# One decoder layer on one core: a new unit order, each engine's sequence written anew, and no filler matmuls

## The chip, the core and the metric

The kernel runs on one core of a Trainium2 chip. A core has a matrix engine (TensorE, PE in the profile), a vector engine (VectorE, DVE), a scalar engine (ScalarE, ACT), a general engine (GpSimd, POOL) and a queue that only starts transfers (SyncE, SP). Each engine executes its own instructions in the order in which they are written, and waits for another engine only through a semaphore. The metric is the device time of one launch in microseconds (us).

## The reference

The input has 8 batches of 128 tokens with 256 features. Three sublayers follow one another, each with a residual sum and a layer norm:

```python
x = layernorm(x + attn(x, Wq, Wk, Wv, Wo))       # 16 heads of 128, 4 key/value heads, rotary positions
x = layernorm(x + xattn(ctx, ctx, x, filt, D))   # long convolution of k*v, multiplied by x as the query
x = layernorm(x + ffn(x, W_gate, W_qkv))         # 16 heads of 16, gated top-1 key and value, causal

# attn: q, k, v = x@W.T; rotary on q, k; softmax(q k / sqrt(128)) v; out @ Wo.T
# xattn: kv[i,j] = k_i * v_j per head; y = causal_conv(kv[i,j], filt) + kv*D; out_j = sum_i y[i,j]*q_i
# ffn: indicator = one_hot(argmax(gate)); k_s = indicator.k; v_s = top1.v; softmax(q k_s) v_s
```

The second sublayer of a batch needs the convolutions of all 16 of its heads (the table `y36`) and the finished first sublayer of that batch. The attention does not depend on the convolutions.

## The kernel before

**Units.** The attention is cut into 8 units. A unit is one group of 4 heads with its key/value head (4 groups) for one half of the batches (2 halves of 4 batches). The order is group 0 half 0, group 0 half 1, group 1 half 0, and so on. The four units that add to the first half's residual are therefore units 0, 2, 4 and 6, and its first layer norm comes after unit 6 of 0 to 7.

**What a unit does.** While unit u attends, TensorE computes the projections of unit u+1: `K`, `Q0` to `Q3`, `V`, each 6 matmuls of 512 columns (L377), since operands are split into a high and a low fp32r part. ScalarE copies a projection rotated (`rot`, L854 and L855), VectorE multiplies by the cosine (L1113) and adds (L1126), GpSimd multiplies by the sine (L1574). Per batch k of the unit, TensorE makes `scores` (L408), VectorE takes the row maximum (L1189), ScalarE exponentiates (L888), GpSimd multiplies by the inverse sum (`normalize`, L1605), TensorE transposes (`turn`, L497), multiplies by the values (`values`, L514 to L519, and L510 in the last unit) and by the output weights (`output`, 12 matmuls, L532). VectorE adds the result to `x` (`accumulate`, L1219).

**Convolutions.** They are Toeplitz matmuls (L394), 4 for each unit (`C0` to `C3`), placed among the unit's projections. Projections and convolutions take turns in two PSUM banks (`proj_bank`), so each waits until the one before the last has been read out. GpSimd makes the products `kv` (L1564) and ScalarE copies the results into `y36` (L872).

**Second and third sublayer.** Per batch b: `x1_turn` (L624) transposes the normed x, ScalarE copies it (`mix_query`, L988), 15 `pair_products` (L318, L321) multiply `y36` by it, VectorE sums them (`mix_sum`, L1376), `mix_turn` (L634) transposes back, VectorE adds and norms (`add_mix`, the norm steps L1352 to L1366 with a power on GpSimd, L1667), `x2_turn` (L642) transposes, then `gate_project`, `kv_project`, `query_project`, the gating on VectorE (`gating`, `share`), `key_turn` (L676), `fscores` (L688, L693), row maximum (L1430), exponentials (L1025), `fturn` (L704), `fvalues` (L714), `y_turn` (L752) and the last norm. After the eight units a function `seq(i)` lists what every engine does for step i, in which three or four batches are in work at different stages.

**Around the end of the attention.** Unit 7 has no next unit, so it has only the convolutions `C1` to `C3` and no projections. Into it the first steps of batches 0 to 3 are woven. For batch 0 the pair products are shared: the near distances (`CLOSE`, `NEXT`) on VectorE, the others on GpSimd. There `keep_busy(n)` issues n matmuls of 512 columns on a constant tile (L417), whose results nobody reads: 5, 6, 2, 5 and 6 of them in unit 7 and 2 after it, and 13 more at the very start.

**What sets the order.** Everything is an order written out by hand: a body of one unit per engine, run eight times by `phase_a`, and the steps of `seq(i)`.

```python
                    output(1)
                    values(2)
                    turn(3)
                    x1_turn(2, 0)
                    keep_busy(6)
                    mix_turn(0, 0)
                    values(3)
                    output(2)
                    x2_turn(0, 0)
```

## Time and profile before

| | before |
|---|---|
| time, median of 3 runs | 339.44 us (336.38 to 342.62) |
| span of the profiled execution | 334.2 us |
| median minus that span | 5.2 us |
| TensorE busy | 316.0 us (95%) |
| VectorE, ScalarE, GpSimd busy | 253.1 us, 232.3 us, 198.7 us |
| mean granted TensorE clock | 0.991 |

The span runs from the first to the last instruction of the one profiled execution. A time of its own is not given for that execution; what the launch takes around the span is read as the difference to the median of the runs. An engine's busy time counts execution alone, so the rest of the span is waiting. The profile models the ends of matmuls: a stretch in which PE is busy throughout has no gap between matmuls.

### The profile page before, as it was taken

The numbers are of one execution on the slowest core, as the hardware profiler recorded it, in microseconds if no ns is written. First come the engines' busy times: TensorE is split into PE (matmuls) and PEld (weight loads), VectorE is DVE, ScalarE is ACT, GpSimd is POOL, SyncE is SP. The second block draws the span as 40 slices with busy tenths as digits, with TensorE's granted clock in tenths as the row PEclk, the third lists the DMA queues.
The fourth block names the chain that finished last, engine by engine and source line by source line (L and its number), as shares of the span: only waits on it lengthen the run. The fifth ranks groups of instructions, "written<-read, shape, count | busy, mean of one in ns | idle before, by whom it ended". The sixth has DMA issues, their size and how long they took to land.

```text
span 334.2 us, 6299 instructions
## 1 busy us (share of the span) xinstructions
PE 316.0 (95%) x2099; PEld 245.1 (73%) x2099; DVE 253.1 (76%) x505; ACT 232.3 (69%) x691; POOL 198.7 (59%) x284
## 2 busy tenths in 40 slices
PE   6998999999999999999999999999699999999982
PEld 2786798898898888888889888755366566666641
DVE  2698867857867856876865776989877899998646
ACT  3679578768868957968867865531458777878781
POOL 0679835837844857754665763799790866812102
PEclk9999999999999999999999999999979999999998
DMA  6941010042010031010040000000000000000010
GB/s 178 352 194 63 2 33 0 1 127 66 0 31 0 3 127 64 0 33 0 0 138 4 1 0 2 1 2 1 0 1 2 2 16 3 17 19 18 1 33 31
DMA packets 5616, 13.08 MB, mean 39 GB/s; under 512 B 848, under 2 KB 3024, under 8 KB 5328
## 3 DMA queue, kind: packets, MB, share of 16 engines
q1 hardware_dynamic: 5312, 12.29, 11.0%
q10 hardware_dynamic: 272, 0.39, 0.4%
q8 instruction: 17, 0.28, 0.3%
q14 instruction: 15, 0.12, 0.1%
HBM read 11.63 MB, written 1.05 MB: 38 GB/s over the span
## 4 chain that ended last, share of the span: by engine, by line
PE 77%; DVE 8%; POOL 6%; issue 3%; ACT 2%; DMA 2%; POOLq 0%; DVEq 0%
PE bank L377 19%; PE bank L532 11%; PE bank L408 8%; PE bank L394 6%; PE bank L704 4%; PE bank L693 4%; PE bank L497 4%; PE bank L659 3%; POOL q_rope L318 3%; PE bank L519 3%; PE bank L714 2%; POOL q_rope L321 2%; PE bank L514 2%; PE bank L516 2%; PE bank L688 2%
## 5 line engine op out<-in xcount | busy, mean ns | idle before, releaser
L1605 POOL TENSOR_TENSOR prob<-prob,rden 128x512 f32<-128x512 f32 x32 | 34.1, 1066 | 46.3 <-DVE rden L1196 46.3
L1574 POOL TENSOR_TENSOR t_sin<-rot,sin 128x512 f32<-128x512 f32 x36 | 46.5, 1298 | 22.4 <-ACT rot L855 21.8
L888 ACT ACTIVATE prob<-bank,neg_max 128x128 f32<-128x128 f32 x128 | 45.4, 373 | 0.8 <-DVE neg_max L1189 0.7
L532 PE MATMUL bank<-wo_hi,head_hi 128*128 128x256 f32 x128 | 38.4, 300 | 1.2 <-POOL wo_lo L1599 0.8
L1025 ACT ACTIVATE prob<-bank,fneg_max 128x128 f32<-128x128 f32 x128 | 36.8, 381 | 2.2 <-DVE fneg_max L1430 2.2
L532 PE MATMUL bank<-wo_hi,head_lo 128*128 128x256 f32 x128 | 36.0, 281 | 0.0
L532 PE MATMUL bank<-wo_lo,head_hi 128*128 128x256 f32 x128 | 36.0, 281 | 0.0
L932 ACT CAST head_hi<-bank 128x512 fp32r<-128x512 f32 x32 | 18.8, 588 | 23.9 <-PE bank L519 15.8
L1564 POOL TENSOR_TENSOR kv<-ctxT 128x256 f32<-128x256 f32 (+3 forms) x64 | 35.2, 579 | 0.0
L377 PE MATMUL bank<-x_hi,w_hi 128*128 128x512 f32 x96 | 31.5, 409 | 2.8 <-DVE w_hi L1155 2.0
L408 PEld LDWEIGHTS bank<-k_rope,q_rope 128*128 128x128 f32 x240 | 31.3, 191 | 2.6
L1113 DVE TENSOR_TENSOR t_cos<-bank,cos 128x512 f32<-128x512 f32 x36 | 24.7, 687 | 11.1 <-ACT rot L855 10.5
L318 POOL TENSOR_TENSOR q_rope<-y,rot 128x64 f32<-128x64 f32 (+7 forms) x61 | 31.8, 527 | 2.0 <-ACT rot L988 2.0
L1667 POOL TENSOR_TENSOR rstd<-var_eps,half_pow 128x1 f32<-128x1 f32 (+1 forms) x18 | 10.9, 607 | 36.1 <-DVE var_eps L1361 33.1
L408 PE MATMUL bank<-k_rope,q_rope 128*128 128x128 f32 x240 | 31.6, 274 | 0.0
L1249 DVE TENSOR_TENSOR head_lo<-bank,head_hi 128x512 fp32r<-128x512 f32 x32 | 22.1, 690 | 11.7 <-ACT head_hi L932 11.2
L854 ACT COPY rot<-bank 64x512 f32<-64x512 f32 x40 | 23.4, 585 | 10.6 <-PE bank L377 8.7
L377 PE MATMUL bank<-x_lo,w_hi 128*128 128x512 f32 x96 | 30.0, 394 | 0.3 <-DVE x_lo L1138 0.3
L377 PE MATMUL bank<-x_hi,w_lo 128*128 128x512 f32 x96 | 30.0, 394 | 0.1
L1189 DVE TENSOR_REDUCE neg_max<-bank 128x4 f32<-128x512 f32 x32 | 22.0, 687 | 9.8 <-PE bank L408 9.5
L394 PE MATMUL bank<-kv,toep 128*128 128x288 f32 x96 | 27.2, 405 | 0.0
L1126 DVE TENSOR_TENSOR q_rope<-t_cos,t_sin 128x512 f32<-128x512 f32 x28 | 23.2, 850 | 5.1 <-POOL t_sin L1574 5.1
(132 smaller groups left out, 814.6 us busy)
## 6 DMA issues: line engine op xcount, KB each, us to landing
w_raw<-in_wqkv SPq DMA_DIRECT2D x3, 768.0 KB, 5.9
toep<-in_toep SPq DMA_DIRECT2D x8, 256.0 KB, 3.1
wo_raw<-in_wo SPq DMA_DIRECT2D x4, 512.0 KB, 3.5
x_raw<-in_xt SPq DMA_DIRECT2D x2, 512.0 KB, 5.5
ctxT<-in_ctx SPq DMA_DIRECT2D x1, 1024.0 KB, 4.8
x<-in_x SPq DMA_DIRECT2D x1, 1024.0 KB, 8.9
out<-x SPq DMA_DIRECT2D x8, 128.0 KB, 1.7
wf<-in_wf SPq DMA_DIRECT2D x1, 784.0 KB, 4.5
```

The costliest lines, as they stand in the source:

```text
L318: last = eng.tensor_tensor(pr[:, :, d * HD:d * HD + (n - 1) * (HD + 1) + 1:HD + 1], y[:, :, at:at + n], q[:, :, 0:n], ALU.mult)
L377: last = pe.matmul(out[:, :], wp[:, c, col:col + P], xp[:, j, c, :], start=(c + n == 0), stop=(c == C - 1 and n == 2))
L394: last = pe.matmul(out, toep[:, j, hh, tap:tap + P], kv[:, j, m, hh * NB:(hh + 1) * NB, :], start=(m == 0), stop=(m == lb))
L408: last = pe.matmul(score_bank[k % 2][:, h * P:(h + 1) * P], q_rope[:, j, h, k * P:(k + 1) * P], k_rope[:, j, k * P:(k + 1) * P], start=Tru ...
L532: last = pe.matmul(acc_bank[k // 2][:, (k % 2) * D:(k % 2 + 1) * D], hp[:, k % 2, h * P:(h + 1) * P], wp[:, v % 2, h, :], start=(h + n == ...
L854: act.copy(rot[0:H2, par, :], bank_in[H2:P, :])
L888: last = act.activation(prob[:, k % 2, h * P:(h + 1) * P], score_bank[k % 2][:, h * P:(h + 1) * P], ACT.Exp, bias=neg_max[:, k % 2, h:h + ...
L1025: last = act.activation(prob[:, c % 2, h * P:(h + 1) * P], scored[:, h * P:(h + 1) * P], ACT.Exp, bias=fneg_max[:, c, h:h + 1])
L1113: dve.tensor_tensor(t_cos[:, par, :].rearrange("p (b t) -> p b t", b=BH), bank_in[:, :].rearrange("p (b t) -> p b t", b=BH), cos[:, :].uns ...
L1564: last = pool.tensor_tensor(kv[:, buf, :, :, at:at + n], src[:, :, :, 0:n], src[:, :, :, d:HD], ALU.mult)
L1574: pool.tensor_tensor(t_sin[:, par, :].rearrange("p (b t) -> p b t", b=BH), rot[:, par, :].rearrange("p (b t) -> p b t", b=BH), sin[:, :].u ...
L1605: pool.tensor_tensor(own, own, rden[:, k % 2, :].unsqueeze(2).to_broadcast([P, HG, P]), ALU.mult).then_inc(norm_done, 1)
```

## The change

**The order of the units.** `GROUP_OF` and `HALF_OF` name group and half of each unit. The first half's units are now 0, 2, 4 and 5, so its sums are complete after unit 5; the second half's are 1, 3, 6 and 7. Group 2 is used in unit 4 and again in unit 7, so its projection weights are loaded and split a second time (`W_LOADS`, 5 loads for 4).

**The convolutions.** `CONVS_OF` gives the units 4, 5, 5, 5, 6 and 6 convolutions, beside the first, and the units 6 and 7 none. They still share the two banks.

**The fillers.** The 26 filler matmuls at the end of the attention are gone; the 13 at the start stay.

**The products.** All pair products of all batches are on GpSimd. Their buffer for even batches is the place of `kv`, the copied query `qmix` has a buffer of its own, and the first two `x1_turn` write to another PSUM bank than the later ones.

**The sequences.** The loops are gone. Each engine's whole program is a list of some 370 (TensorE), 320 (ScalarE), 360 (VectorE) and 150 (GpSimd) steps. Steps of batches 0 to 2 now stand in units 6 and 7.

```diff
+GROUP_OF = [0, 0, 1, 1, 2, 3, 3, 2]
+HALF_OF = [0, 1, 0, 1, 0, 0, 1, 1]
+HALF_ENDS = [5, 7]
+W_LOADS = [0, 1, 2, 3, 2]
+W_SPLIT_IN = {0: 1, 2: 2, 3: 3, 5: 4}
-BODY = ["K", "Q0", "Q1", "Q2", "Q3", "C1", "C2", "C3", "C0", "V"]
-LAST = ["C1", "C2", "C3"]
+CONVS_OF = [range(1, 5), range(5, 10), range(10, 15), range(15, 20), range(20, 26), range(26, 32),
+            range(32, 32)]
+ITEMS = [ROPED_ITEMS + [f"C{n}" for n in convs] + ["V"] for convs in CONVS_OF]
-        prod = q_rope[:, :, :, :].rearrange("p n h t -> p n (h t)").rearrange(
-            "p n (a j i) -> p n a j i", j=HD, i=HD)
+        prod = [own.rearrange("p (a j i) -> p a j i", j=HD, i=HD) for own in (
+            kv[:, :, :, :, :].rearrange("p n c a m -> p (n c a m)")[:, 0:C * XH * HD * HD],
+            q_rope[:, 0, :, :].rearrange("p h t -> p (h t)"))]
-        qmix = rot[:, :, 0:D]
+        qmix = sb("qmix", [P, 2, D])
...
-                    values(2)
-                    turn(3)
-                    x1_turn(2, 0)
-                    keep_busy(6)
-                    mix_turn(0, 0)
+            x1_turn(0)
+            values(6, 1)
+            scores(6, 3)
+            turn(6, 2)
+            output(6, 0)
+            output(6, 1)
+            scores(7, 0)
+            x1_turn(1)
+            scores(7, 1)
+            values(6, 2)
+            turn(6, 3)
+            item(6, "V")
+            scores(7, 2)
+            v_turn(7)
+            values(6, 3)
+            output(6, 2)
+            mix_turn(0)
+            turn(7, 0)
+            output(6, 3)
```

**Two places in the order.** TensorE, unit 7, around the transpose `mix_turn` of batch 0 (L634). Before (L510 `values`, L497 `turn`, L624 `x1_turn`, L417 fillers):

```order
L510 MATMUL bank5<-probT,v_last 128x512
L497 MATMUL bank4<-ident,prob 128x128 x4
L624 MATMUL bank0<-ident,x 128x128 x2
L417 MATMUL bank3<-filler 128x512 x6
L634 MATMUL bank0<-ident,t_cos 128x128 x2
```

After, what stands from `scores(7, 0)` (L438) to the transpose of the new values (L411); `mix_turn` of batch 0 comes after 15 more matmuls:

```order
L438 MATMUL bank2<-k_rope,q_rope 128x128 x4
L576 MATMUL bank7<-ident,x 128x128 x2
L438 MATMUL bank3<-k_rope,q_rope 128x128 x4
L527 MATMUL bank5<-probT_hi,v_hi 128x512
L529 MATMUL bank5<-probT_hi,v_lo 128x512
L532 MATMUL bank5<-probT_lo,v_hi 128x512
L509 MATMUL bank4<-ident,prob 128x128 x4
L401 MATMUL bank1<-x_hi,w_hi 128x512 x2
L401 MATMUL bank1<-x_lo,w_hi 128x512 x2
L401 MATMUL bank1<-x_hi,w_lo 128x512 x2
L438 MATMUL bank2<-k_rope,q_rope 128x128 x4
L411 MATMUL bank1<-ident,vT 128x128 x4
```

Between batch 0's `x1_turn` and its `mix_turn` stood fillers and unit 7's steps; now it is the second half of unit 6 with the last projection.

VectorE, from the pair products of batch 0 to their sum (`mix_sum`, L1376). Before (L1189 and L1196 row maximum and inverse, L1249 `head_low`, L1236 copy of the turned probabilities):

```order
L1196 RECIPROCAL rden<-den 128x4
L1345 TENSOR_SCALAR x<-x,mean_var1,rstd1 128x256
L1249 TENSOR_TENSOR head_lo<-bank5,head_hi 128x512
L1236 COPY probT<-bank4 128x512
L318 TENSOR_TENSOR q_rope<-y36,rot 128x32x6
L321 TENSOR_TENSOR q_rope<-y36,rot 128x32x6
L1376 TENSOR_REDUCE t_cos<-q_rope 128x256
L1249 TENSOR_TENSOR head_lo<-bank5,head_hi 128x512
```

After:

```order
L1743 TENSOR_SCALAR x<-x,mean_var1,rstd1 128x256
L1673 TENSOR_REDUCE neg_max<-bank3 128x4
L1680 RECIPROCAL rden<-den 128x4
L1696 TENSOR_TENSOR x<-bank6,x 128x512
L1722 TENSOR_TENSOR head_lo<-bank5,head_hi 128x512
L1715 TENSOR_TENSOR probT_lo<-bank4,probT_hi 128x512
L1780 TENSOR_REDUCE t_cos<-kv 128x256
L1722 TENSOR_TENSOR head_lo<-bank5,head_hi 128x512
```

The sum of batch 0 now stands among steps of unit 6, and no product is left on VectorE.

## Rows read from the trace of the kernel before

**Rows 1.** The page: span, busy time by engine, granted clock in 40 slices.

```profile
span 334.2 us, 6299 instructions
...
PE 316.0 (95%) x2099; PEld 245.1 (73%) x2099; DVE 253.1 (76%) x505; ACT 232.3 (69%) x691; POOL 198.7 (59%) x284
...
PEclk9999999999999999999999999999979999999998
```

**Rows 2.** Windows: length, then busy us (instructions) by engine, clock, DMA.

```profile
49.99:178.80 128.81, 128.81 (x802) 112.52 (x801) 94.39 (x160) 98.73 (x287) 78.48 (x87) 1.00 0.12 38
178.80:233.04 54.24, 52.93 (x318) 41.02 (x317) 43.92 (x87) 30.37 (x100) 41.04 (x65) 1.00 0.01 1
233.04:251.00 17.96, 14.38 (x91) 9.37 (x92) 14.52 (x34) 8.98 (x31) 15.33 (x32) 0.90 0.01 1
...
242.00:246.00 4.00, 4.00 (x18) 3.23 (x16) 2.99 (x10) 1.98 (x7) 4.00 (x10) 0.60 0.00 0
...
284.00:317.00 33.00, 33.00 (x278) 20.91 (x277) 28.10 (x72) 26.34 (x84) 11.70 (x24) 1.00 0.04 14
```

**Rows 3.** Windows again, the filler matmuls of line L417 alone (PE, then PEld).

```profile
178.80:233.04 54.24, 6.60 (x26) 2.47 (x26) 1.00 0.01 1
```

**Rows 4.** The chain that ended last: start us, us, what, in order of time.

```profile
49.99 1.39 PE bank L377 x6
...
110.97 1.40 PE bank L377 x6
112.37 0.89 PE bank L408 x8
113.96 1.46 PE bank L394 x6
115.85 1.42 PE bank L532 x12
...
178.80 1.39 PE bank L377 x6
```

**Rows 5.** Timeline of PE around the attention's end: start, us, instruction, idle before.

```profile
213.86 1.24 PE L417 MATMUL bank<-filler 128*128 128x512 bf16 x5
215.47 0.38 PE L532 MATMUL bank<-wo_hi,head_hi 128*128 128x256 f32 x1 [0.37 <-DVE head_lo L1249]
...
233.04 0.59 PE L688 MATMUL bank<-causal,identb 128*128 128x512 bf16 x2
...
241.50 0.44 PE L624 MATMUL bank<-ident,x 128*128 128x128 f32 x2 [2.33 <-DVE x L1345]
...
248.98 0.44 PE L642 MATMUL bank<-ident,x 128*128 128x128 f32 x2 [0.77 <-DVE x L1366]
```

**Rows 6.** Timeline of DVE in unit 7: batch 0's products on VectorE.

```profile
211.85 1.82 DVE L318 TENSOR_TENSOR q_rope<-y,rot 128x256 f32<-128x256 f32 x2
213.50 0.90 DVE L321 TENSOR_TENSOR q_rope<-y,rot 128x224 f32<-128x224 f32 x1
...
215.94 0.78 DVE L318 TENSOR_TENSOR q_rope<-y,rot 128x192 f32<-128x192 f32 x1
216.55 1.30 DVE L321 TENSOR_TENSOR q_rope<-y,rot 128x192 f32<-128x192 f32 x1
```

**Rows 7.** Costliest groups: line, operation, tiles, count | busy us, mean ns | idle before.

```profile
L1605 POOL TENSOR_TENSOR prob<-prob,rden 128x512 f32<-128x512 f32 x32 | 34.1, 1066 | 46.3 <-DVE rden L1196 46.3
...
L318 POOL TENSOR_TENSOR q_rope<-y,rot 128x64 f32<-128x64 f32 (+7 forms) x61 | 31.8, 527 | 2.0 <-ACT rot L988 2.0
...
L1113 DVE TENSOR_TENSOR t_cos<-bank,cos 128x512 f32<-128x512 f32 x36 | 24.7, 687 | 11.1 <-ACT rot L855 10.5
...
L1126 DVE TENSOR_TENSOR q_rope<-t_cos,t_sin 128x512 f32<-128x512 f32 x28 | 23.2, 850 | 5.1 <-POOL t_sin L1574 5.1
...
L1376 DVE TENSOR_REDUCE t_cos<-q_rope 128x256 f32<-128x2048 f32 x8 | 18.2, 2275 | 0.0
```

**Rows 8.** Timeline, the last instruction before the final transfer.

```profile
331.70 0.41 DVE L1366 TENSOR_SCALAR x<-x_raw,mean_var,rstd 128x256 f32<-128x256 f32 x1 [0.44 <-POOL rstd L1667]
```

More of the change, by code:

```diff
@@ new lines, in _ @@
+            scores(1, 0)
+            item(0, "C4")
+            item(0, "V")
+            turn(0, 3)
+            output(0, 2)
+            scores(1, 1)
+            values(0, 3)
+            v_turn(1)
+            item(1, "K")
+            scores(1, 2)
+            item(1, "Q0")
+            turn(1, 0)
+            scores(1, 3)
+            item(1, "Q1")
+            output(0, 3)
+            turn(1, 1)
+            values(1, 0)
+            item(1, "Q2")
+            item(1, "Q3")
+            turn(1, 2)
@@ new lines, in _ @@
+            scores(2, 3)
+            item(2, "Q2")
+            item(2, "Q3")
+            output(1, 2)
+            values(2, 0)
+            turn(2, 1)
+            output(1, 3)
+            item(2, "C10")
+            item(2, "C11")
+            values(2, 1)
+            turn(2, 2)
+            item(2, "C12")
+            scores(3, 0)
+            item(2, "C13")
+            values(2, 2)
+            turn(2, 3)
+            output(2, 0)
+            item(2, "C14")
+            item(2, "V")
@@ new lines, in _ @@
+            output(6, 3)
+            values(7, 0)
+            turn(7, 1)
+            scores(7, 3)
+            x2_turn(0)
+            turn(7, 2)
+            values(7, 1)
+            output(7, 0)
+            gate_project(0)
+            values(7, 2)
+            output(7, 1)
+            turn(7, 3)
+            query_project(0)
+            x1_turn(2)
+            kv_project(0, 0)
+            mix_turn(1)
+            kv_project(0, 1)
+            values(7, 3)
+            output(7, 2)
+            key_turn(0)
@@ new lines, in _ @@
+            output(7, 3)
+            x2_turn(1)
+            fscores(0, 0)
+            gate_project(1)
+            x1_turn(3)
+            kv_project(1, 0)
+            kv_project(1, 1)
+            fturn(0, 0)
+            fscores(0, 1)
+            mix_turn(2)
+            fturn(0, 1)
+            fvalues(0, 0)
+            query_project(1)
+            key_turn(1)
+            fturn(0, 2)
+            x1_turn(4)
+            fscores(1, 0)
+            x2_turn(2)
+            fvalues(0, 1)
@@ new lines, in _ @@
+            fturn(0, 3)
+            fvalues(0, 2)
+            gate_project(2)
+            x1_turn(5)
+            fscores(1, 1)
+            fturn(1, 0)
+            kv_project(2, 0)
+            mix_turn(3)
+            kv_project(2, 1)
+            fvalues(0, 3)
+            query_project(2)
+            fturn(1, 1)
+            y_turn(0)
+            key_turn(2)
+            fvalues(1, 0)
+            fscores(2, 0)
+            x2_turn(3)
+            fturn(1, 2)
+            fvalues(1, 1)
@@ new lines, in _ @@
+            gate_project(3)
+            fturn(1, 3)
+            x1_turn(6)
+            fvalues(1, 2)
+            kv_project(3, 0)
+            fturn(2, 0)
+            fscores(2, 1)
+            fvalues(1, 3)
+            kv_project(3, 1)
+            mix_turn(4)
+            query_project(3)
+            fturn(2, 1)
+            y_turn(1)
+            key_turn(3)
+            fvalues(2, 0)
+            fturn(2, 2)
+            fscores(3, 0)
+            x2_turn(4)
+            fvalues(2, 1)
@@ new lines, in _ @@
+            fvalues(2, 2)
+            gate_project(4)
+            fturn(2, 3)
+            x1_turn(7)
+            kv_project(4, 0)
+            fturn(3, 0)
+            fscores(3, 1)
+            fvalues(2, 3)
+            kv_project(4, 1)
+            query_project(4)
+            mix_turn(5)
+            fturn(3, 1)
+            y_turn(2)
+            key_turn(4)
+            fvalues(3, 0)
+            fscores(4, 0)
+            x2_turn(5)
+            fturn(3, 2)
+            fvalues(3, 1)
@@ new lines, in _ @@
+            gate_project(5)
+            fvalues(3, 2)
+            kv_project(5, 0)
+            fturn(3, 3)
+            fscores(4, 1)
+            fturn(4, 0)
+            kv_project(5, 1)
+            fvalues(3, 3)
+            query_project(5)
+            mix_turn(6)
+            fturn(4, 1)
+            key_turn(5)
+            fvalues(4, 0)
+            y_turn(3)
+            fscores(5, 0)
+            x2_turn(6)
+            fturn(4, 2)
+            fvalues(4, 1)
+            gate_project(6)
@@ new lines, in _ @@
+            fturn(4, 3)
+            kv_project(6, 0)
+            fvalues(4, 2)
+            fscores(5, 1)
+            fturn(5, 0)
+            kv_project(6, 1)
+            fvalues(4, 3)
+            query_project(6)
+            mix_turn(7)
+            fturn(5, 1)
+            key_turn(6)
+            fvalues(5, 0)
+            y_turn(4)
+            fscores(6, 0)
+            x2_turn(7)
+            fturn(5, 2)
+            fvalues(5, 1)
+            gate_project(7)
+            fvalues(5, 2)
```

1972 lines of the change are left out of this document (1299 added, 673 removed).

## The prediction

> **What bounds the kernel now.** I read the page first: TensorE is busy for 316.0 of 334.2 us, all other engines for 76% or less [rows 1]. That share alone doesn't say that TensorE is the limit in every stage, so I cut the span into windows at places the chain gives. From 49.99 to 178.80 us, which are units 1 to 5 (the K projection of unit 1 and that of unit 6 [rows 4]), TensorE is busy for 128.81 of 128.81 us [rows 2]: 25.76 us a unit, no gap, and the chain runs through its matmuls. Nothing but less TensorE work can shorten this stage. The steady part of the later sublayers is of the same kind: 33.00 of 33.00 us from 284 to 317, with VectorE at 28.10 (85%) [rows 2]. What is left are the start, the end, and the passage between the two stages. In the passage, from 178.80 to the first `fscores` at 233.04 [rows 5], TensorE is busy for 52.93 of 54.24 us [rows 2], but 6.60 us of that are 26 fillers whose results nobody reads [rows 3]. They stand in front of waits: the five at 213.86 are followed by 0.37 us of idleness for VectorE's `head_lo` [rows 5]. The useful work is 52.93 - 6.60 = 46.3 us, and 7.9 us are lost. In the next stretch, to 251.00, TensorE is busy for 14.38 of 17.96 us: 3.6 us idle, of which 2.33 us wait for the norm of batch 4 and 0.77 us for that of batch 2 [rows 2, 5]. Behind the long wait the clock falls, to 0.60 over 242 to 246 [rows 2], so that 1.6 us of those 4 are lost as well. **The whole passage loses 7.9 + 3.6 + 1.6 = 13.1 us. That is what the change can give back.**
>
> **The passage, first part.** The same work stands there as before, less 7 convolutions (C1 to C3 of unit 6, C0 to C3 of unit 7, 22 matmuls), which move ahead. Six take 1.46 us on the chain [rows 4], so 22 take 5.4 us, which are paid in units 0 to 5 instead and cancel. That leaves 46.3 - 5.4 = 40.9 us for TensorE. VectorE had 43.92 us there [rows 2] and loses the products of batch 0, 1.82 + 0.90 + 0.78 + 1.30 = 4.8 us [rows 6], so it has 39.1 us, 96% of TensorE's. In the steady stage 85% went with no wait at all, and before, the passage ran at 43.92 / 54.24 = 81% with 7.9 us lost; 96% in order, with every fourth or fifth step waited for, will not be free. GpSimd gets those products: a batch's 15 cost it about 15 x 0.527 = 7.9 us by the mean of the dearer kind [rows 7], and one `normalize` of 1.07 stands between them [rows 7]. With the sum on VectorE, 2.28 us [rows 7], the path from `x1_turn` to `mix_turn` of batch 0 is 7.9 + 1.1 + 2.3 = 11.3 us, and copies and handovers. TensorE has as cover three `output` (4.3 us), four `scores` (3.6), one projection (1.4) [rows 4], three `values` and four short transposes, together some 12.8 us if I put those seven at half a us each. Cover and path are equal to within about a us, so a small wait is likely there, and another at `key_turn` of batch 0, where gating and `share` on VectorE have only 2 `kv_project`, a `values` and one `output` over them. Bounds of what comes back as new waits: nothing (the 40.9 us are dense) and all 7.9 us. I take 3.0, nearer to dense, since the products leave VectorE and real work replaces the fillers. **Term: -4.9 us.**
>
> **The passage, second part.** The second half's statistics now stand on VectorE ahead of the first `fscores` maximum, not behind it, and `x1_turn` of batch 4 stands behind three `fturn` and two `fscores`. The wait of 2.33 us [rows 5] and the slow clock behind it lose their cause. But `key_turn` of batch 1 waits for `gating` and `share` that stand behind a sum of 2.28 us. Bounds: -5.2 and 0. I take 1.7 back. **Term: -3.5 us.**
>
> **The dense units.** Before, units 1 to 5 had no wait, so here the new order can only lose. A convolution or projection needs its bank free, which took two `rot` copies and a cosine product of 0.69 us [rows 7] behind the projection before the last, against one projection of 1.40 us in between [rows 4]: two projections back to back with none between wait, and in the new list they stand in pairs with a `scores` or `turn` between the pairs, as before. Total work rises by 5.4 us of convolutions over these units, with the same share of the other engines. The trace has no such unit. The low bound is 0. For the high one I take 1 us a unit over six, the size of the wait for the norm [rows 5]. Nearest is the stage itself, with none in 128.81 us [rows 2]. **Term: +1.0 us.**
>
> **Edits at nothing.** The fifth weight load is hidden: its split costs ScalarE and VectorE under 2 us each in unit 5, where VectorE had 94.39 of 128.81 us to do over five units [rows 2]; if the cover fails, it is 2 us of wait. The load itself has a unit of 25.76 us to land in. SyncE's queue carries it behind two Toeplitz loads, which wait for convolutions that are now early. The start has the same steps in another order, and the tail's last chain ends in the same apply at 331.70 [rows 8]; its norms of batches 6 and 7 only swap with a short scale. I put both at 0, with 1 us either way.
>
> **A rule that speaks against it: the clock.** The trace shows full speed through all of the fillers, and 0.60 only behind the 2.33 us of idleness [rows 2, 5]. The Trainium skill ("TensorE: Matmul & The Clock Gate", Part 1) puts it as "the default state is throttled, and activity releases the throttle", so fillers have a use of their own. By the trace alone, waits of up to 0.37 us leave the clock up [rows 5], and mine are of 1 us or less, so the sum has nothing for it; by the rule, a spell of waits costs as one below does.
>
> **Another: the port.** VectorE's cosine product reads PSUM and SBUF and takes 687 ns; the addition (L1126) reads SBUF twice and takes 850 ns [rows 7]. That difference is there while GpSimd works beside it. The Trainium skill ("SBUF — State Buffer", Who interferes with whom) says that a tensor_tensor with both inputs in SBUF contends with GpSimd's reads. By the rows, five additions of unit 6 beside busier GpSimd work cost 5 x 0.16 = 0.8 us at most more, which is inside the 3.0 us; by the rule, each could wait for a whole product of 0.5 us, 2.6 us in all.
>
> **The sum.** -4.9 - 3.5 + 1.0 = -7.4 us on a span of 334.2: 326.8 us. The median of the runs lies 5.2 us above that span, so the time is 339.44 - 7.4 = 332.0 us, 2.2% less. A measurement of this kernel can tell about 2%, 6.8 us, from no change; the forecast lies on that line.
>
> **Rivals.**
> (a) *Everything comes back.* The sum of losses is 13.1 us, and nothing new arises. For it: GpSimd and ScalarE have room, and the first half's residual is complete a unit earlier. Against it: VectorE at 96%. With at most 1 us of new waits the time is 339.4 - 12.1 = 327.3.
> (b) *The gain turns into new waits.* VectorE is the passage's engine, and units with six convolutions wait for banks. Then 3 of the 13.1 us stay gained by the passage's two parts, after all 7.9 and 2 us return, and the dense units lose another 2: 339.4 - 3.2 + 2 = 338.2. For it: a list in order with each engine over 90% has no slack, and the dense stage has nothing to win. This is also the case in which the change removes the fillers and not what they covered.
> (c) *Slower: the clock.* One mechanism: at the passage, waits without fillers between them bring TensorE to 1.2 GHz, as at 242 us. One such fall costs its wait of 2.3 and 1.6 us of slow work, 3.9 us. It starts to decide when a wait gets as long as the 2.33 us one; four falls between units 6 and batch 2, with (b)'s waits, give 339.4 - 1.2 + 15.6 = about 354, two give 346. Against it: the waits that I find are about 1 us.
>
> **How the numbers follow.** The forecast (332, itself between 329 and 335.5) has 0.47, (a) 0.15, (b) 0.30, (c) 0.08. Faster by over 2% means below 332.6: all of (a) and 0.34 of the forecast, 0.49. Within 2%: the rest of the forecast and (b), 0.43. Slower by over 2%: (c), 0.08. The range leaves out half of (c) and the ends of (a) and (b): 326 to 341.
>
> **What would show it.** Right: no idleness of TensorE over 1.2 us between K of unit 6 and the first `fscores`, that stretch 43 to 45 us long; units 1 to 5 dense in TensorE, 134 us with their convolutions; clock 1.00 after 240 us. Wrong in the first term: VectorE busy throughout with TensorE waiting for `head_lo` or the turned probabilities. Wrong in the third: waits for cosine products or `rope` sums in units 1 to 5. Wrong in the clock: slices under 9 in the passage. What would upset all is work that I take as equal and isn't: the steady stage's 33.00 of 33.00 us would have to become longer.

## The result, and the profile after

| | before | after |
|---|---|---|
| time, median | 338.5 us (20 runs, 335.99 to 342.78) | 339.5 us (20 runs, 338.26 to 342.06) |
| ratio to before, 95% interval | | 1.006 (1.003 to 1.008) |
| span of the profiled execution | 334.2 us | 336.5 us |
| TensorE busy | 316.0 us | 312.7 us |
| VectorE, ScalarE, GpSimd busy | 253.1, 232.3, 198.7 us | 262.9, 231.3, 204.7 us |

The forecast of 332.0 us and its sign were wrong: the time rose by 0.6%, which the 20 runs of each tell apart from no change, and which is far inside 2%. Rival (b), 338.2 us, comes nearest by the time. A run's time is 1.8 to 1.9 us longer than its own span in every run that lists both (338.36 and 336.5 us for the profiled execution of after). So the profiled execution of before, 334.2 us of span, was one of its fastest; the profiled one of after is among its fastest too, and the two spans, 2.2 us apart, can be compared.

The page of after (span, busy time, granted clock, the chain by engine) answers to [rows 1]:

```profile
span 336.5 us, 6269 instructions
...
PE 312.7 (93%) x2073; PEld 241.0 (72%) x2073; DVE 262.9 (78%) x502; ACT 231.3 (69%) x693; POOL 204.7 (61%) x289
...
PEclk9999999999999999999999999999999999999997
...
PE 36%; DVE 23%; issue 15%; POOL 14%; ACT 8%; DMA 3%; POOLq 0%; DVEq 0%; ACTq 0%
```

The slow slice of before (7, near 242 us) is gone, as forecast. But VectorE has become 9.8 us busier although the change takes five instructions of batch 0's products (4.8 us [rows 6]) off it, and GpSimd, VectorE and "issue" hold half of the chain.

Windows of after, at the places of [rows 2], the first of them without a gap in before and with 5.0 us of idle TensorE now (length, then busy us and instructions by engine, clock, DMA):

```profile
51.15:193.53 142.38, 137.37 (x837) 117.68 (x836) 106.57 (x168) 103.63 (x305) 86.23 (x94) 1.00 0.12 40
193.53:239.05 45.52, 43.08 (x270) 35.03 (x269) 41.32 (x80) 26.06 (x86) 36.08 (x55) 1.00 0.01 2
239.05:257.00 17.95, 17.32 (x123) 10.54 (x122) 17.04 (x39) 12.99 (x45) 17.16 (x38) 1.00 0.01 1
```

I cut both traces at the same work: the first matmul of a unit's K projection, and the first `fscores`. Of before these cuts lie at 49.83, 178.64 and 233.04 us. 22 matmuls of convolutions count 5.35 us [rows 4], and in after one `output` (12 matmuls, 1.42 us [rows 4]) still stands behind the cut at 51.15.

| stretch | before | after | moved work | left over | forecast |
|---|---|---|---|---|---|
| start and unit 0 | 49.83 | 51.15 | -1.42 | +2.7 | 0 |
| units 1 to 5 | 128.81 | 142.38 | +6.77 | +6.8 | +1.0 |
| passage to the first `fscores` | 54.40 | 45.52 | -5.35 | -3.5 | -4.9 |
| from there to the end | 101.20 | 97.44 | 0 | -3.8 | -3.5 |
| sum | 334.2 | 336.5 | 0 | +2.2 | -7.4 |

So the passage did what it was to do, 7.3 of the forecast 8.4 us. Ahead of it 9.5 us were lost where 1.0 was expected. Of the 6.8 us in units 1 to 5, 5.0 are idle time of TensorE (142.38 - 137.37); the rest lies inside its busy time. What TensorE waited for in after, whole span (us in total, times, the longest):

```profile
PE bank L423 <- DVE t_cos L1594: 2.3, 3, 1.0
PE bank L438 <- DVE q_rope L1607: 2.2, 3, 1.2
PE bank L470 <- POOL q_rope L2295: 1.6, 2, 1.1
...
PE bank L401 <- DVE t_cos L1594: 1.4, 4, 0.5
PE bank L401 <- DVE x_lo L1620: 1.3, 1, 1.3
```

Convolutions (L423) wait for cosine products, scores (L438) for sums: the words of the prediction for "wrong in the third". And the groups, as in [rows 7]:

```profile
L2287 POOL TENSOR_TENSOR t_sin<-rot,sin 128x512 f32<-128x512 f32 x36 | 47.3, 1324 | 29.8 <-ACT rot L1128 24.0 <-DVE q_rope L1607 3.5 <-DVE k_rope L1607 2.1
L2315 POOL TENSOR_TENSOR prob<-prob,rden 128x512 f32<-128x512 f32 x32 | 35.5, 1114 | 49.4 <-DVE rden L1680 49.4
L1607 DVE TENSOR_TENSOR q_rope<-t_cos,t_sin 128x512 f32<-128x512 f32 x28 | 33.4, 1214 | 1.8 <-POOL t_sin L2287 1.7
...
L1594 DVE TENSOR_TENSOR t_cos<-bank,cos 128x512 f32<-128x512 f32 x36 | 24.3, 683 | 7.5 <-ACT rot L1128 6.7
```

The same 28 sums went from 850 to 1214 ns, 10.2 us more of VectorE; the cosine product, with one input in PSUM, stayed at 683. With K's eight there are 36 sums. I sorted them by what GpSimd did meanwhile: before, 16 ran beside nothing and took 0.69 us, after only 3; beside a sine product alone 12 of after took 1.28 in the mean, beside `kv` alone 9 took 0.97. The longest took 2.03 us before and 2.40 in after, both beside GpSimd's `wo_lo`.

**One place in full.** The longest pair of waits, in unit 3. TensorE, VectorE and GpSimd of after (start, us, instruction, idle before):

```profile
119.73 1.24 PE L423 MATMUL bank<-kv,toep 128*128 128x288 f32 x4 [0.96 <-DVE t_cos L1594]
121.70 0.75 PE L423 MATMUL bank<-kv,toep 128*128 128x288 f32 x2 [0.73 <-DVE t_cos L1594]
```

```profile
114.55 0.68 DVE L1594 TENSOR_TENSOR t_cos<-bank,cos 128x512 f32<-128x512 f32 x1
115.16 0.67 DVE L1722 TENSOR_TENSOR head_lo<-bank,head_hi 128x512 fp32r<-128x512 f32 x1
115.75 1.63 DVE L1634 SCALAR_TENSOR_TENSOR toep<-anti,dcoef,toep 128x128 f32<-128x128 f32 x2
117.34 1.74 DVE L1607 TENSOR_TENSOR q_rope<-t_cos,t_sin 128x512 f32<-128x512 f32 x1
119.00 0.68 DVE L1594 TENSOR_TENSOR t_cos<-bank,cos 128x512 f32<-128x512 f32 x1
119.72 1.33 DVE L1607 TENSOR_TENSOR q_rope<-t_cos,t_sin 128x512 f32<-128x512 f32 x1
120.97 0.68 DVE L1594 TENSOR_TENSOR t_cos<-bank,cos 128x512 f32<-128x512 f32 x1
```

```profile
113.17 2.74 POOL L2277 TENSOR_TENSOR kv<-ctxT 128x160 f32<-128x160 f32 x5
115.86 2.68 POOL L2287 TENSOR_TENSOR t_sin<-rot,sin 128x512 f32<-128x512 f32 x2
119.22 1.27 POOL L2287 TENSOR_TENSOR t_sin<-rot,sin 128x512 f32<-128x512 f32 x1 [0.69 <-DVE q_rope L1607]
```

C15 needs the bank that Q2's cosine product frees. That product (119.00) stands behind the skip matrices and behind Q1's sum. The sum waits for nothing more, but runs beside a sine product and takes 1.74 us. The sines are late because `kv` (2.74 us) stands ahead of them. VectorE works without a gap here, on steps nobody is waiting for yet, while TensorE waits. Three candidates are left, two in these rows and one beside them: the **order** on VectorE and GpSimd (theory A), the **port** that two engines share (theory P), and that five or six convolutions in a unit are too many wherever they stand (theory C).

### The profile page after: what moved, and what is told of

Read it like the earlier page. It is cut to its first block, busy times and chain, and to the rows that moved or that the text cites. A ratio compares the mean times of both kernels' runs of the same rounds, so it can differ in the third digit from the quotient of the medians.

```text
span 336.5 us, 6269 instructions
## 1 busy us (share of the span) xinstructions
PE 312.7 (93%) x2073; PEld 241.0 (72%) x2073; DVE 262.9 (78%) x502; ACT 231.3 (69%) x693; POOL 204.7 (61%) x289
## 4 chain that ended last, share of the span: by engine, by line
PE 36%; DVE 23%; issue 15%; POOL 14%; ACT 8%; DMA 3%; POOLq 0%; DVEq 0%; ACTq 0%
PE bank L401 5%; DVE q_rope L1607 5%; PE bank L548 5%; PE bank L423 4%; ACT prob L1163 4%; PE bank L438 4%; DVE t_cos L1594 2%; POOL kv L328 2%; PE bank L659 2%; PE bank L617 2%; POOL t_sin L2287 2%; DVE head_lo L1722 2%; PE bank L670 2%; POOL kv L331 2%; ACT rot L1128 2%
## 5 line engine op out<-in xcount | busy, mean ns | idle before, releaser
L2315 POOL TENSOR_TENSOR prob<-prob,rden 128x512 f32<-128x512 f32 x32 | 35.5, 1114 | 49.4 <-DVE rden L1680 49.4
L2287 POOL TENSOR_TENSOR t_sin<-rot,sin 128x512 f32<-128x512 f32 x36 | 47.3, 1324 | 29.8 <-ACT rot L1128 24.0
L401 PE MATMUL bank<-x_hi,w_hi 128*128 128x512 f32 x96 | 33.0, 425 | 3.4 <-DVE w_hi L1641 1.5
L1607 DVE TENSOR_TENSOR q_rope<-t_cos,t_sin 128x512 f32<-128x512 f32 x28 | 33.4, 1214 | 1.8 <-POOL t_sin L2287 1.7
L438 PE MATMUL bank<-k_rope,q_rope 128*128 128x128 f32 x240 | 31.5, 276 | 2.2 <-DVE q_rope L1607 2.2
L438 PEld LDWEIGHTS bank<-k_rope,q_rope 128*128 128x128 f32 x240 | 29.9, 191 | 4.6 <-DVE q_rope L1607 3.5
L2277 POOL TENSOR_TENSOR kv<-ctxT 128x256 f32<-128x256 f32 (+7 forms) x64 | 33.1, 553 | 0.0
L401 PE MATMUL bank<-x_lo,w_hi 128*128 128x512 f32 x96 | 29.9, 393 | 1.3 <-DVE x_lo L1620 1.3
L423 PE MATMUL bank<-kv,toep 128*128 128x288 f32 x96 | 27.6, 410 | 2.5 <-DVE t_cos L1594 2.3
L401 PE MATMUL bank<-x_hi,w_lo 128*128 128x512 f32 x96 | 29.8, 392 | 0.0
L1163 ACT ACTIVATION_READ_ACCUMULATOR prob<-bank,neg_max 128x1 f32 x128 | 27.3, 213 | 0.0
L548 PEld LDWEIGHTS bank<-wo_hi,head_hi 128*128 128x128 f32 x128 | 24.1, 189 | 3.5 <-DVE head_lo L1722 2.0
```

The lines of the kernel that those rows point to most:

```text
L401: last = pe.matmul(out[:, :], wp[:, c, col:col + P], xp[:, j, c, :], start=(c + n == 0), stop=(c == C - 1 and n == 2))
L423: last = pe.matmul(out, toep[:, j, hh, tap:tap + P], kv[:, j, m, hh * NB:(hh + 1) * NB, :], start=(m == 0), stop=(m == lb))
L438: last = pe.matmul(score_bank[k % 2][:, h * P:(h + 1) * P], q_rope[:, j, h, k * P:(k + 1) * P], k_rope[:, j, k * P:(k + 1) * P], start=Tru ...
L548: last = pe.matmul(acc_bank[k // 2][:, (k % 2) * D:(k % 2 + 1) * D], hp[:, k % 2, h * P:(h + 1) * P], wp[:, g % 2, h, :], start=(h + n == ...
L1163: last = act.activation(prob[:, k % 2, h * P:(h + 1) * P], score_bank[k % 2][:, h * P:(h + 1) * P], ACT.Exp, bias=neg_max[:, k % 2, h:h + ...
L1607: dve.tensor_tensor(dst, t_cos[:, par, :], t_sin[:, par, :], ALU.add).then_inc(rope_done, 1)
```

## The experiments

Times are medians; the ratio is to runs of the kernel before, made beside them on the same chip. "Units 1 to 5" is K of unit 1 to K of unit 6. At before's density they take 128.81 + 5.35 = 134.2 us with the seven convolutions; after has 142.38 - 1.42 = 141.0.

### 1. The change's steps in before's unit

The same steps as after, each as often: its unit order, convolutions, and its lists from unit 6 on. The start and units 0 to 5 are written in the pattern of before's unit, on all four engines, TensorE included. Unit 3 on VectorE, after (-) and mixture (+):

```diff
-prob_low 0; cos K; cos Q0; prob_low 1; add K; add Q0; cos Q1; head_low 0; add_skip 4; add Q1; cos Q2;
-add Q2; cos Q3; accumulate; add Q3; head_low 1; row_max 3
+cos K; prob_low 0; row_max 2; cos Q0; head_low 0; add K; add Q0; cos Q1; add Q1; invert 2; add_skip 4;
+cos Q2; prob_low 1; row_max 3; cos Q3; head_low 1; add Q2; add Q3
```

> The same steps as in the changed kernel, in another order up to the end of unit 5: the start and units 0 to 5 follow the unit body of the kernel before (with the extra convolutions put between its own), units 6 and 7 and all behind them are those of the changed kernel. Theory A (the new order of the dense units and of the start makes the waits): units 1 to 5 go from 142.4 us back to about 134, the start and unit 0 give back 2 to 3 us, the passage stays at 45.5; span 336.5 - 10 = 326 to 328. Rival (five or six convolutions in a unit, or the new unit order with its fifth weight load, cost the time whatever the order): units 1 to 5 stay above 139, span 332 to 336.

Measured: 340.75 us, ratio 1.005 (0.999 to 1.011), span 336.4; no gain. But the loss sat elsewhere. The start was back at before's (K of unit 1 at 49.64), the mean sum fell from 1.197 to 0.942 us, and units 1 to 5 took 143.8 us with two waits of convolutions that had not been in after:

```profile
95.54 0.72 PE L423 MATMUL bank<-kv,toep 128*128 128x288 f32 x2 [1.82 <-issue]
...
180.62 1.30 PE L423 MATMUL bank<-kv,toep 128*128 128x288 f32 x2 [2.80 <-issue]
```

"issue" names no releaser. On GpSimd five `kv` products run from 178.70 to 180.51, until just before C28 at 180.62: C12 and C28 begin new pairs (3 and 7), whose `kv` products I had placed too late. This run didn't decide between A and C.

### 2. The same with three placements mended

```diff
 # GpSimd
-unit 2: normalize(3, 0), pairs(4)      unit 5: pairs(7, 0:3), normalize(5, 3), pairs(7, 3:)
+unit 2: pairs(4), normalize(3, 0)      unit 4: pairs(7), normalize(5, 0)
 # TensorE and ScalarE, unit 2: C12 a slot later, then C13 and C14 behind values(2, 3)
```

> The kernel before's way of laying out a unit for the start and units 0 to 5, with the change's distribution of the convolutions, and the change's lists for units 6, 7 and behind. It differs from the first such mixture only in where GpSimd's kv products of pairs 4 and 7 stand (a unit's tail earlier) and in one convolution of unit 2 that stands a slot later. Theory A (the order of the steps inside a unit causes the loss, no property of more convolutions in fewer units): the two waits of 1.82 us at 95.5 and 2.80 us at 180.6 go, and what followed them; from K of unit 1 to K of unit 6 it takes 134.5 to 136.5 us, against 140 in the first mixture, span 330 to 332, ratio to before 0.988. Theory C (six convolutions in a unit leave VectorE or the banks behind, wherever they stand): the same waits turn up at other places, 139 to 141 us, span 335 to 336, ratio 1.00.

Measured: 332.42 us, ratio 0.985 (0.979 to 0.991), span 330.6, as A had them. Both waits were gone. Units 1 to 5 took 137.8 us, 3.6 over full density and midway between A's and C's figures; the "140" that the expectation gives for the first mixture was a slip for 143.8, on which C's figure hung. From K of unit 6 to the end it equals after to within 0.2 us (143.1 and 143.0). **So three placements inside the units are worth 6.0 us, and after's own steps in this order take 5.9 us less of span than in after's (330.6 for 336.5), where after had lost 2.2 us against before: order is the larger part of what was lost.** Against after, 2.9 us of it lie at the start and in unit 0 and 3.2 in units 1 to 5 (141.0 to 137.8); 0.2 go back behind them. The order of every engine differs between the two, so this doesn't say which engine's counted. C isn't dead: 3.6 us remained, of which TensorE is idle for 1.7 (137.80 - 136.12).

```profile
49.70:187.50 137.80, 136.12 (x825) 116.37 (x823) 100.01 (x166) 103.73 (x298) 83.58 (x96) 1.00 0.13 42
187.50:233.05 45.55, 43.06 (x270) 35.03 (x269) 41.31 (x80) 27.18 (x92) 36.02 (x55) 1.00 0.00 1
```

### 3. The port alone: one swap

In experiment 2 one VectorE split ran beside a GpSimd one, both on SBUF alone:

```profile
131.26 2.40 POOL L2309 TENSOR_TENSOR wo_lo<-wo_raw,wo_hi 128x1024 fp32r<-128x1024 f32 x1 [4.53 <-ACT wo_hi L1114]
...
131.95 2.52 DVE L1620 TENSOR_TENSOR w_lo<-w_raw,w_hi 128x768 fp32r<-128x768 f32 x1 [0.99 <-ACT w_hi L1108]
```

```diff
 # ScalarE, end of unit 3
-split_wo(2)
 split_w(3, 1)
+split_wo(2)
```

> The second mixture with one swap in ScalarE's list: at the end of unit 3 it splits the projection weights (w_hi) ahead of the output weights (wo_hi), so that VectorE's w_lo no longer runs beside GpSimd's wo_lo. In the second mixture this one w_lo took 2.52 us beside GpSimd's 2.40 us one, where the eleven others took 0.95 to 1.09, and the values of unit 4 then waited 0.16 and 0.40 us for the turned probabilities, on either side of a late t_cos. Theory P (two engines on SBUF operands at once cost VectorE the difference, and that cost reaches TensorE where a step is waited for soon): this w_lo takes 0.95 to 1.1 us, unit 4 takes 27.5 to 28.3 us for 28.96, K of unit 1 to K of unit 6 136.4 to 137.2 us for 137.8, span 329.2 to 330.0. Rival (the 2.52 us are only a coincidence of a busy DMA or of the weights' own arrival): w_lo stays above 2 us. Second rival (the time is absorbed by slack): w_lo is short and unit 4 stays at 28.8 to 29.0.

```profile
131.00 0.96 DVE L1620 TENSOR_TENSOR w_lo<-w_raw,w_hi 128x768 fp32r<-128x768 f32 x1
...
131.99 2.40 POOL L2309 TENSOR_TENSOR wo_lo<-wo_raw,wo_hi 128x1024 fp32r<-128x1024 f32 x1 [5.26 <-ACT wo_hi L1114]
```

Measured: 331.67 us, ratio 0.983 (0.978 to 0.989), span 329.8; unit 4 took 28.25 us for 28.96. The split fell from 2.52 to 0.96 us, the level of the other w_lo splits (nine, not the eleven of the expectation; 0.95 to 1.08 us). So P is shown as the cause of those 1.6 us of VectorE's time. Of what TensorE got, 0.7 us, it isn't the only cause: the swap also starts the split 0.95 us sooner, so it ends 2.5 us sooner (131.96 for 134.47), and the two weren't separated. By its span this is the fastest of all kernels here, ahead of before (334.2) and after.

### 4. The port taken out of the sums

The cosine product goes back to its PSUM bank and the sum reads it there, so the sum has one SBUF input. The bank is then held until the sum.

```diff
-dve.tensor_tensor(t_cos[:, par, :]..., bank_in, cos, ALU.mult)
-dve.tensor_tensor(dst, t_cos[:, par, :], t_sin[:, par, :], ALU.add)
+dve.tensor_tensor(bank_in[:, :]..., bank_in, cos, ALU.mult)
+dve.tensor_tensor(dst, bank_in[:, :], t_sin[:, par, :], ALU.add)
```

> The changed kernel, but the cosine product is written back into its PSUM bank and the addition reads it there, so it has one input in SBUF and not two; the bank comes free behind the addition and not behind the cosine product. Port theory: additions of 690 ns with GpSimd busy beside them or not, VectorE 10 to 12 us less busy, units 1 to 5 down from 142.4 to 137 or less, unless the banks held longer (0.7 us and more each) take it back. Order theory: nothing gained, and the longer hold costs; units 1 to 5 at 142 to 150.

```profile
L1609 DVE TENSOR_TENSOR q_rope<-bank,t_sin 128x512 f32<-128x512 f32 x28 | 18.5, 681 | 1.6 <-POOL t_sin L2289 1.6
```

Measured: 381.84 us, ratio 1.134 (1.125 to 1.143). All sums are short (681 ns for 1214) beside the same GpSimd work, so the second SBUF input is what lengthens them. The time says how much more a held bank costs than a long sum: units 1 to 5 took 171.2 us, where neither theory had more than 150. TensorE waited for banks behind K's and the queries' sums 14 times on L401 alone (16.0 + 13.8 us), and the clock's mean fell to 0.947. The Trainium skill ("SBUF — State Buffer", Who interferes with whom) says that a VectorE instruction with two SBUF inputs contends with a GpSimd instruction that reads SBUF, and that one with at most one, outside VectorE's two-port modes, doesn't; the runs agree, 0.66 to 0.69 us for all 36 sums here against up to 2.40 us in after.

### 5. Less, and more, on GpSimd

After, with only the shortest `kv` product of each pair from pair 2 on (the other products, and so part of the second sublayer's result, are left out):

```diff
                 for d in ...:
+                    if n >= 2 and d < HD - 1:
+                        continue
```

> The changed kernel with less work on GpSimd in units 1 to 5: of the eight kv products of each convolution pair from the third on, only the shortest is computed (the second sublayer's result is not the reference's). Nothing else moves. Port theory (VectorE's additions with both inputs in SBUF are held up by GpSimd's work): the mean addition falls from 1214 ns to 1000 or less, and units 1 to 5 lose part of their waits, 142.4 to 139 or 140. Order theory (VectorE's steps simply stand late in the list, or banks come free late): additions change, but units 1 to 5 stay within 1 us of 142.4.

Measured: 337.77 us, ratio 1.002 (0.998 to 1.006), span 334.8; mean sum 1.109 us for 1.197, units 1 to 5 1.5 us shorter. Most of `kv` out of the way gives back 1.5 of the 6.8 us, a little beyond the order theory's 1 us and short of P's figures (a mean of 1.0 or less, 139 to 140 us). Most of what stayed of the collisions is with the sines.

Before, with the products of distance 2 and more made a second time:

```diff
+                    if d >= 2:
+                        pool.tensor_tensor(kv_again[..., at - 15:at - 15 + n], src[..., 0:n], src[..., d:HD], ALU.mult)
```

> The kernel before, in which GpSimd makes its kv products of distance 2 and more a second time into a tile that nobody reads: GpSimd is busier beside the same VectorE work, TensorE's order is untouched. Theory P (VectorE's additions of two SBUF tiles are lengthened by GpSimd's tensor_tensor beside them): the mean addition rises from 0.87 to 1.0 us or more. Whether that alone costs the dense units time: by P as the whole cause, units 1 to 5 grow from 25.76 to 26.5 us each or more and the span to 338 or more; by A, with the addition's slack in before's order, they stay within 0.2 us of 25.76 wherever GpSimd's own work isn't late, and the span stays within 1.5 us.

Measured: 347.78 us, ratio 1.030 (1.023 to 1.037), span 347.4, units 0.9 and 1.6 us longer by turns, unit 0 5.5. The mean sum stayed at 0.88 us, so this doesn't bear on P, and my expectation of 1.0 failed: the extra products stood where VectorE made no sums. What grew was another thing, 8.2 us of idleness before the convolutions (L395), where before had none: 0.9 of it the profile puts down to `kv`, and 7.3 to "issue", which names no releaser. That these too are waits for `kv` is likely, not shown. Before's unit has no room for 21 us more of GpSimd (219.9 us for 198.7), though GpSimd was busy for 59%.

### 6. Single moves in after's unit 3

The place shown above, C15 and C16, 1.69 us of waits:

```diff
 # e_cos_ahead, VectorE
 cos Q1; head_low 0
+cos Q2
 add_skip 4; add Q1
-cos Q2; add Q2; cos Q3
+cos Q3; add Q2
 # e_kv_behind, GpSimd
-pairs(4, 3:); sin Q1; sin Q2
+sin Q1; sin Q2; pairs(4, 3:)
```

> The changed kernel with one cosine product moved, in unit 3 alone: VectorE makes Q2's ahead of the skip matrices and Q1's sum, and Q3's ahead of Q2's sum. In the changed kernel C15 waits 0.96 us and C16 0.73 us here for these two products, which stand behind the skip matrices (1.63 us) and a sum of 1.74 us. Theory A (what TensorE waits for stands behind what nobody is waiting for): t_cos of Q2 comes at 115.8 us instead of 119.0, C15 doesn't wait, C16 waits 0.4 us or less, K to K of unit 3 takes 24.00 - 0 us or 31.84 - 1.3 = 30.5 us whichever of the two stretches holds the wait, all together 1.2 to 1.7 us less to K of unit 4. Rival: VectorE, at 4.00 of 4.00 us from 114 to 118, is the limit whatever its order, and the wait turns up at the next head_lo or sum; then less than 0.5 us is gained by K of unit 4.

> The changed kernel with GpSimd's five kv products of pair 4 (2.74 us at 113.17) moved behind the sine products of Q1 and Q2 of unit 3, VectorE's list untouched. By theory A the sines come 1.5 us earlier, ScalarE's wait of 1.60 us for t_sin goes, and the sum of Q1 no longer runs beside a sine product (1.74 us), but it still stands behind the skip matrices: C15 waits 0.3 us, C16 up to 0.5, together 0.8 to 1.1 us gained by K of unit 4. By theory P in the strict form (the duration of the sum decides) the sum falls to 0.7 to 1.0 us and the gain is its whole difference, 0.7 to 1.0. Rival: no gain, or a loss of up to 1 us, since C16 needs these kv products, which now end at 119.8.

> Both of the two moves before, together in unit 3. If the two remove the same wait, 1.4 to 1.7 us gained by K of unit 4, little more than the cosine move alone; if they are independent, the two gains add up, to at most the 1.69 us of waiting that is there. VectorE's sum of Q1 beside the kv products: 0.9 to 1.1 us.

One execution each, so unit lengths are compared, not times: K of unit 3 to K of unit 4 takes 24.00 us in after, 23.52 with the cosine move (-0.48), 23.08 with the `kv` move (-0.92), 23.06 with both. Units 1, 2, 4 and 5 were equal to within 0.02 us. The spans were 336.1, 338.0 and 337.7 us; the last two had a slow clock at the start (below). The cosine move is a miss: C15's wait went, C16's fell to 0.30, and a new one arose behind it:

```profile
119.98 0.75 PE L423 MATMUL bank<-kv,toep 128*128 128x288 f32 x2 [0.30 <-DVE t_cos L1594]
...
122.36 1.16 PE L438 MATMUL bank<-k_rope,q_rope 128*128 128x128 f32 x8 [0.93 <-DVE q_rope L1607]
```

The rival's figure came, less than 0.5 us. Its reason, that VectorE is the limit whatever its order, is only in part borne out: VectorE has no gap here, but an `accumulate` nobody waits for still stands ahead of the sum that TensorE now waits for, and the skip matrices take 2.24 us for 1.63, beside sine products in both kernels. The `kv` move does what was expected of it, 0.92 us. The sines come earlier, and the sum no longer runs beside one (0.94 us for 1.74); how much of the 0.92 is due to each isn't separated. Together the moves give 0.94 us where 1.4 to 1.7 was expected, so the second adds next to nothing to the first.

### 7. The start, and the fillers

After, with `split_x(1)` put back behind the rotations (ScalarE) and the first row maximum (VectorE):

> The changed kernel with one thing put back: ScalarE's and VectorE's split of the second half of x stands again behind the first rotations and the first row maximum, as before. Theory A (the order of the steps on ScalarE and VectorE at the start makes the start longer): K of unit 0 ends its wait and unit 1's K starts 1.3 to 2 us earlier, K to K of unit 0 13.8 to 14.5 us for 15.9; the rest unchanged; span 334.5 to 335.5. Theory C (the start is longer by the convolution that unit 0 has more): K to K stays at 15.5 to 16 us.

Measured: 338.83 us, ratio 1.004 (1.001 to 1.007), the first K to K of unit 0 15.91 us, as in after (15.94). The waits of 0.55 and 1.10 us for GpSimd went, and one of 1.37 us for VectorE's `q_rope` took their place. The length is the one theory C gave, but the next run shows that C's reason, the added convolution, isn't it. Then with ScalarE's `split_wo(0)` behind the first exponentials too, and all of VectorE's start:

```diff
-split_w(0,0); split_x(0); split_w(0,1); cos K; add K; cos Q0; cos Q1; add_skip 0; cos Q2; split_x(1); cos Q3; row_max
+split_x(0); split_w(0,0); split_w(0,1); cos K; cos Q0; add K; cos Q1; cos Q2; cos Q3; add_skip 0; row_max; split_x(1)
```

> The changed kernel with the whole start of before put back on ScalarE and VectorE: x_lo ahead of w_lo, the cosine product of Q0 ahead of K's sum, the skip matrices and the split of x's second half behind the four cosine products. Theory A (the order of these steps is the start's whole loss, 0.96 us at x_lo and some 1.4 at the first scores): K to K of unit 0 13.8 to 14.0 us for 15.94, and the 1.9 to 2.1 us are kept to the end: span 334.4 to 334.8. Rival (what is gained at the start is lost again in units 0 to 5, since their waits are for VectorE and GpSimd and not for TensorE): K of unit 6 comes less than 0.8 us earlier, span 335.7 to 336.5.

Measured: 13.80 us, as before: 2.1 of the 2.7 us are the order of these steps. But the time was 338.24 us, ratio 1.002 (0.998 to 1.006), and the span 336.6. In the profiled execution 1.5 us of the gain stood until K of unit 3 (106.18 for 107.69) and were gone at K of unit 4. The waits there were the same, 0.94 and 0.72 us, yet this time the clock fell. Windows, first the two of after, then of this run:

```profile
118.00:122.00 4.00, 2.31 (x12) 1.54 (x11) 3.96 (x5) 3.17 (x5) 1.81 (x2) 1.00 0.01 4
122.00:126.00 4.00, 4.00 (x31) 3.67 (x30) 3.04 (x6) 1.86 (x7) 0.00 (x0) 1.00 0.23 64
```

```profile
118.00:122.00 4.00, 3.04 (x8) 2.10 (x9) 3.30 (x5) 2.08 (x5) 0.99 (x1) 0.78 0.23 68
122.00:126.00 4.00, 4.00 (x27) 3.81 (x27) 2.48 (x4) 1.84 (x8) 0.00 (x0) 0.79 0.00 0
```

A mean of 0.78 is a part of the window at 1.2 GHz; the clock fell behind the second wait, after 120 us. It cost 1.6 us (25.60 us from K of unit 3 to K of unit 4 for 24.00), all that was left of the start's gain. It isn't so in each execution: four of this kernel's ten have spans of 334.8 to 335.1 us at a mean clock of 0.993 or more, near the 334.4 to 334.8 that theory A gave, and after's own at such a clock have 336.4 to 336.8. So with the clock up some 1.5 us of the start's order reach the end.

Before, without its 26 fillers at the attention's end:

```diff
-keep_busy(5) ... keep_busy(6) ... keep_busy(2) ... keep_busy(5) ... keep_busy(6)
```

> The kernel before without its 26 filler matmuls at the end of the attention, that part of the change alone. If the fillers only stood in front of waits: the same time within 1 us, the clock no lower. If they keep the clock up: a granted clock well under 1.00 somewhere between 214 and 235 us and 2 to 5 us more. If they cost: 1 to 3 us less.

Measured: 336.77 us, ratio 0.999 (0.995 to 1.004), span 333.1; the passage took 53.35 us for 54.40. The waits show where the fillers had been: 1.53 us for `head_lo` where 0.37 stood [rows 5], then 1.50 and 1.29 us for the sums of the products, and the clock stayed at 1.00.

```profile
178.38:231.81 53.43, 47.75 (x293) 38.92 (x292) 43.22 (x85) 30.59 (x100) 39.99 (x62) 1.00 0.01 1
```

## Why the prediction was wrong, by its own steps

**What bounds the kernel: right.** TensorE bounds units 1 to 5 of before, and only the passage had something to give. Experiment 3 confirms that there was a prize: a list that keeps the units nearly dense gives 329.8 us of span, 4.4 less than before, where I had 7.4.

**Passage, first part (-4.9): -3.5, mechanism right.** The dense work of 40.9 us came out too low. Without fillers TensorE is busy for 47.75 us over the same stretch, so they held only about 5 us of it, and the work is 47.75 - 5.35 = 42.4 us; after shows 43.08. New waits were 2.4 us where I had 3.0, the longest for TensorE 0.63. That a window's busy time can't be taken apart by subtracting groups was what I missed: the term was mis-sized by 1.5 to 2.2 us of work. VectorE had 41.32 us where I had 39.1, and the stretch took 45.52 us, just over the 43 to 45 named for "right".

**Passage, second part (-3.5): -3.8, right.** The 2.33 us wait and the slow clock are gone; the clock reads 1.00 from 239 to 257.

**Dense units (+1.0, bounds 0 and 6): +6.8. This step failed.** I wrote that the change leaves "the same share of the other engines" and that projections "stand in pairs with a scores or turn between the pairs, as before", and took the stage's own row, no wait in 128.81 us, as the nearest. I judged by TensorE's list, and read even that too kindly: it has three convolutions in a row twice, C6 to C8 and C28 to C30, where before has two at most (no wait of theirs is over 0.16 us, so this isn't where the time went). The row of no wait shows what before's *order* on all engines hid, and the change rewrote the order of VectorE and GpSimd too. What TensorE waited for in these units was theirs in all but 0.2 us: cosine products, sums, and steps behind them. Experiments 1 to 3 show that on the same work the loss is 9.7, 3.6 or 2.9 us by where a few steps stand. How much of the 6.8 is the port can't be separated fully: the sums' 10.2 us more of VectorE are there; most of `kv` out of the way gives 1.5, the swap of one split 0.7, and a `kv` move 0.92, each by order and port at once. What remains of 2.9 us in the best list may be C's share; no run tells that.

**The port (at most 0.8 us, in the passage): right rule, wrong place and size.** I priced five sums of unit 6 at the difference of the *means*, 0.16 us. A mean of 850 ns was a mix of 0.69, 0.95 and single ones of up to 2.03; in after a collision costs up to 1.7 us (2.40 for 0.68), and it came in the dense units, where the new lists put the sums beside sines.

**Start (0, 1 us either way): +2.7.** "The same steps in another order" was no reason for nothing: 2.1 us of it are that order (experiment 7). The fifth weight load was hidden as said: units 6 and 7 show no wait for it.

**The clock (0; rival c): right for the fillers and for after.** By experiment 7 removing the fillers alone cost nothing. But to put nothing in the sum because my waits were of 1 us or less was too sure: two of 0.94 to 0.96 and 0.72 to 0.73 us, 1.2 us of work between them, left the clock up in one execution and not in another, at a cost of 1.6 us. The Trainium skill ("TensorE: Matmul & The Clock Gate", Part 1) has it that activity releases the throttle. These traces agree in that the clock fell behind waits (to 0.78 here, 0.60 in [rows 2]), and show beside it that the same steps can go either way.

**From span to time (5.2 us).** I added the difference between the median and one span. A run's own time lies 1.8 to 1.9 us above its span; the other 3.4 us are that the profiled execution was faster than the median of three runs. Of 20 runs the median of before was 338.5, not 339.44.

**The chances.** Rival (b), at 0.30, is nearest to the outcome, and gave as its reason "a list in order with each engine over 90% has no slack". That its time came within 1.3 us is partly luck. It gave the passage a gain of 3.2 us where 7.3 came, the dense units a loss of 2 where 6.8 came, and the start nothing where 2.7 was lost. By the span it gives 334.2 - 1.2 = 333.0 us, and after had 336.5; the median taken for before, 0.9 us too high, hid a part of that.

## What to carry to other kernels

A stage in which the bounding engine never waits has proved its order on *every* engine, not only its work; when a change rewrites the lists, write down for the helpers' engines too what stands ahead of each step that the bound engine is going to wait for, and keep the dense stage's pattern while rewriting only the stage that had losses (a ratio to before of 0.983 here, against 1.006 for the new lists throughout). For a group of one operation and one shape look at the shortest and the longest, not only at the mean: a spread of 0.68 to 2.40 us shows collisions between two engines, and one such was scheduled away here (experiment 3). And a busy engine with a wait beside it isn't yet the limit: read which of its steps nobody needs so soon.

## What the runs showed of the hardware

- VectorE's 128x768 subtraction with both inputs in SBUF took 0.96 us by itself and 2.52 us beside GpSimd's 128x1024 one, which took 2.40 us in both cases: there the whole cost fell on VectorE. The 128x512 sum went from 0.68 to as much as 1.76 us beside GpSimd's products and 2.40 beside that subtraction, and stayed at 0.66 to 0.69 with one input in PSUM.
- The cost can fall on GpSimd too, by which of the two is already running. In after, `wo_lo` began 0.6 us before the end of a VectorE sum twice and took 2.84 and 2.86 us; the same in two other kernels with after's order (experiments 5 and 7). The 22 other such splits in the traces of before, after, experiments 1 to 3, `e_few_pairs` and `e_start` took 2.37 to 2.41.

```profile
87.23 1.52 DVE L1607 TENSOR_TENSOR q_rope<-t_cos,t_sin 128x512 f32<-128x512 f32 x1
...
88.17 2.84 POOL L2309 TENSOR_TENSOR wo_lo<-wo_raw,wo_hi 128x1024 fp32r<-128x1024 f32 x1
```

- The granted clock doesn't follow from a wait's length alone: the same two waits (0.94 to 0.96 and 0.72 to 0.73 us) kept 1.00 in one execution, and in another gave 0.78 over the 4 us around the second and 0.79 over the next 4. Without the fillers, waits of 1.53, 1.50 and 1.29 us within 14 us kept 1.00. At the start, around one of 1.33 us for x_lo, three kernels with after's start have a 9 in the second slice of the clock's row; the two with the `kv` move, whose start is the same, have a 5 and a 6, and were 2.1 and 1.8 us longer by K of unit 0.
